# Two aggregating layers of a graph network: every second tile's hi and lo rows transposed by a DMA instead of TensorE

## What is computed

```python
h = layernorm(x)
for l in range(3):
    h_neigh = segment_sum(h[src], dst, n) / deg
    rst = relu(h @ W_self[l] + h_neigh @ W_neigh[l] + b[l])
    h = rst / max(sqrt(sum(rst * rst)), 1e-12)
x = x + h
x = x + ffn(layernorm(x))     # 8 experts, the best 2 of them by a gate
```

## Time and profile before

| what | value |
|---|---|
| time, median of 3 runs | 2151.08 us (2150.09 to 2151.2) |
| profiled execution, first to last instruction | 2150.1 us |
| PE busy | 2019.1 us (94%) |
| DVE busy | 1710.3 us (80%) |
| POOL busy | 1278.2 us (59%) |
| ACT busy | 1022.8 us (48%) |
| TensorE clock granted, mean | 0.985 of full speed |
| chain that ended last | PE 63%, POOL 11%, DVE 10%, issue 8%, ACT 4%, DMA 3% |

### The profile page before, as it was taken

The page is one execution under the profiler, slowest core; times in us unless marked ns, Lnnn a source line. Parts: engine busy times, 40 slices in busy tenths (PEclk is TensorE's granted clock), DMA queues, the critical chain, the costliest instruction groups (busy, mean ns, idle before and its releaser), DMA issues.

```text
span 2150.1 us, 44050 instructions
## 1 busy us (share of the span) xinstructions
PE 2019.1 (94%) x15237; PEld 1133.0 (53%) x15237; DVE 1710.3 (80%) x4183; ACT 1022.8 (48%) x1794; POOL 1278.2 (59%) x1396
## 2 busy tenths in 40 slices
PE   6999899997999999998999999987699989999996
PEld 3444444443444444443444444443477767777674
DVE  7678986655888888875888888875699989999985
ACT  4444333333334343443343343444677667766651
POOL 2884117664566666553444444444588888888865
PEclk9999999998999999999999999999999999999999
DMA  6664348964555555554666766665788997999874
GB/s 208 167 168 130 123 138 139 139 123 123 174 176 174 172 174 174 173 168 140 217 218 215 220 220 215 213 212 161 195 168 169 172 168 175 171 174 173 173 108 53
DMA packets 246210, 364.12 MB, mean 169 GB/s; under 512 B 115577, under 2 KB 115751, under 8 KB 245991
## 3 DMA queue, kind: packets, MB, share of 16 engines
q1 hardware_dynamic: 185175, 195.88, 35.9%
q0 software_dynamic: 60816, 165.43, 29.8%
HBM read 175.81 MB, written 165.31 MB: 159 GB/s over the span
## 4 chain that ended last, share of the span: by engine, by line
PE 63%; POOL 11%; DVE 10%; issue 8%; ACT 4%; DMA 3%; another core or an unknown queue 0%; SPq 0%; DVEq 0%; POOLq 0%; ACTq 0%
PE psS L523 26%; PE psY L523 25%; PE psT L1726 4%; POOL out_dram L861 2%; PE psY L1822 2%; POOL node_info L696 2%; PE psA L1781 2%; PE psA L1780 1%; POOL X L789 1%; DVE R L1429 1%; DMA w_n<-HH 1%; DMA w_s<-HH 1%; POOL G L773 1%; POOL zr L852 1%; POOL area L773 1%
## 5 line engine op out<-in xcount | busy, mean ns | idle before, releaser
L523 PE MATMUL psY<-w_n,HT 128*128 128x512 f16 x2664 | 616.6, 381 | 11.9 <-ACT HT L926 9.8
L523 PE MATMUL psS<-w_s,HT 128*128 128x512 f16 x2664 | 611.2, 379 | 1.0 <-DVE SB L1320 1.0
L523 PEld LDWEIGHTS psY<-w_n,HT 128*128 128x128 f16 x2664 | 260.7, 98 | 332.1 <-ACT HT L926 14.0
L523 PEld LDWEIGHTS psS<-w_s,HT 128*128 128x128 f16 x2664 | 251.5, 98 | 263.8 <-DVE SB L1320 1.2
L953 ACT ACTIVATE RR<-R 128x512 f32<-128x512 f32 x237 | 149.5, 631 | 303.4 <-DVE R L1429 299.4
L805 POOL DMA_INDIRECT y_rows<-YB,poutT x158 | 161.5, 1022 | 189.9 <-DVE YB L1308 157.9
L1320 DVE SCALAR_TENSOR_TENSOR SB<-psS,downs,bias 128x512 f32<-128x512 f32 x237 | 177.7, 750 | 76.8 <-PE psS L523 65.9
L798 POOL TENSOR_TENSOR scl<-ssm,halfpow 128x1 f32<-128x1 f32 x158 | 88.6, 561 | 239.3 <-DVE ssm L1447 239.2
L523 PE MATMUL psS<-w_w,raw 128*128 128x512 f16 x948 | 219.8, 382 | 0.8 <-ACT raw L1043 0.8
L1308 DVE SCALAR_TENSOR_TENSOR YB<-psY,YB 128x512 f16<-128x512 f32 x237 | 162.5, 686 | 55.6 <-ACT YB L919 46.8
L961 ACT ACTIVATE HH<-RR,scl 128x512 f16<-128x512 f32 x158 | 114.0, 722 | 150.1 <-POOL scl L798 150.1
(11 more groups left out here) (311 smaller groups left out, 3802.4 us busy)
## 6 DMA issues: line engine op xcount, KB each, us to landing
self_rows<-SB SPq DMA_DIRECT2D x236, 256.0 KB
Sl<-self_rows SPq DMA_DIRECT2D x158, 256.0 KB
area<-in_x_dram SPq DMA_DIRECT2D x78, 256.0 KB
y_rows<-YB SPq DMA_DIRECT2D x78, 256.0 KB
out_dram<-obb SPq DMA_DIRECT2D x78, 256.0 KB
raw<-in_L_gnn_W_neigh_dram SPq DMA_DIRECT2D x12, 256.0 KB
raw<-in_L_gnn_W_self_dram SPq DMA_DIRECT2D x12, 256.0 KB
y_rows<-YB,poutT POOLq DMA_INDIRECT x158
```

What stands on the lines that cost most here:

```text
L523: mm = eng.matmul(acc, lhs[:, a, c, :], w[:, bpart, c, :], start=(c == 0 and n == 0), stop=(stop and c == KC - 1 and n == 2))
```

## The change

For l = 1 and 2, an odd tile that is not late is turned by a transposing DMA that SP issues (`turn_rows`), straight from `HH` into one of four SBUF tiles `HTD` (the first four of `HTR`). PE's eight transposes and DVE's copy of that tile fall away. `turn_rows` stands in SP's steps with offset 1, ahead of `store_early`. `neigh` of such a tile waits for the DMA's landing (semaphores `hd`), and so does ACT's `hhi` of two tiles later, which writes the same `HH` buffer. The counts in the other waits are adapted, since PE turns fewer tiles. There are 37 such tiles in l = 1 (1 to 73) and 34 in l = 2 (1 to 67). The core of the diff:

```diff
+HD_RING = 4
+def by_dma(t, l):
+    return l in (1, 2) and t.t % 2 == 1 and late_place(t, l) is None
+def turned_by_dma(t):
+    before = t.run * len([k for k in range(T) if by_dma(Tile(k), 1)])
+    return before + len([k for k in range(t.t + 1) if by_dma(Tile(k), t.run + 1)])
+def turned_by_pe(t, l):
+    return t.n + 1 - (turned_by_dma(t) if l else 0)
...
+        HTD = HTR[0:HD_RING]
+        def dma_slot(t):
+            return (turned_by_dma(t) - 1) % HD_RING
+        def dma_landed(t):
+            return 16 * ((turned_by_dma(t) - 1) // HD_RING + 1)
...
             k = late_place(t, l)
+            if by_dma(t, l):
+                return HTD[dma_slot(t)]
...
+                def turn_rows(t, s=s, l=l):
+                    if not by_dma(t, l):
+                        return
+                    i = t.slot(2)
+                    sp.wait_ge(s.hhi, (t + 1).n)
+                    sp.wait_ge(s.hlo, (t + 1).n)
+                    if turned_by_dma(t) > HD_RING:
+                        sp.wait_ge(s.sp, (t + (1 - 2 * HD_RING)).n if t.t >= 2 * HD_RING else t.run * T)
+                    sp.dma_start_transpose(turned_rows(t, l).rearrange("p a c n -> p (a c) n"),
+                                           HH[i].rearrange("p a n -> p (a n)")).then_inc(s.hd[dma_slot(t)], 16)
-                    run_tiles(T, [(0, store_early)])
+                    run_tiles(T, [(1, turn_rows), (0, store_early)])
...
-                    run_plan(T, [(0, store_early), (5, load_self), (2, out_bias)],
+                    run_plan(T, [(1, turn_rows), (0, store_early), (5, load_self), (2, out_bias)],
...
-                after(act, s.tr, (t + -1).n)
+                if t.t >= 2 and by_dma(t + -2, l):
+                    act.wait_ge(s.hd[dma_slot(t + -2)], dma_landed(t + -2))
+                elif t.n >= 2:
+                    act.wait_ge(s.tr, turned_by_pe(t + -2 if t.t >= 2 else Tile(T - 2 + t.t, t.run - 1), l))
...
-                if late_place(t, l) is not None:
+                if late_place(t, l) is not None or by_dma(t, l):
                     return
...
-                after(pe, s.ht, (t + -1).n)
+                after(pe, s.ht, turned_by_pe(t, l) - (2 if l == 0 or late_place(t, l) else 1))
...
-                pe.wait_ge(s.ht, (t + 1).n)
+                if by_dma(t, l):
+                    pe.wait_ge(s.hd[dma_slot(t)], dma_landed(t))
+                else:
+                    pe.wait_ge(s.ht, turned_by_pe(t, l))
...
-                    if late_place(t, l) is None:
+                    if late_place(t, l) is None and not by_dma(t, l):
                         turn(t, l)
```

More of the change, by code:

```diff
@@ L194, in __init__ @@
         self.ht = sem("ht")
+        self.hd = [sem(f"hd{i}") for i in range(HD_RING)]
         self.y = sem("y")
@@ L971, in turn_late @@
                 s = ph[l]
-                act.wait_ge(s.tr, (t + 1).n)
+                act.wait_ge(s.tr, turned_by_pe(t, l))
                 act.activation(turned_rows(t, l), psT[t.slot(2)][:, :, :, :], ACT.Copy).then_inc(s.ht, 1)
@@ L1298, in turn @@
                 i = t.slot(2)
-                dve.wait_ge(s.tr, (t + 1).n)
+                dve.wait_ge(s.tr, turned_by_pe(t, l))
                 after(dve, s.sp, (t + -1).n)
```

## The result

The changed kernel takes 2498.44 us (median) against 2150.85 us of the kernel before in the same comparison: a ratio of 1.1616, 95% interval 1.1603 to 1.1629. It is 348 us slower. The forecast was 2427 us, slower, with 2275 to 2540 as the range. One of its six executions took 6316.16 us, why is not known, and stands outside the ratio. The profiled execution spans 2496.3 us.

A forecast was written before the change was run, and what follows sets the result against it. PE was taken to bound l = 1 and l = 2. Longer periods (63 + 140 us) and lower clock (26 + 47 us) add 276 us to 2150.1; with the median 1.0 us above the profiled span, 2427 us, range 2275 to 2540.

The forecast's parts named there:

- The ceiling of 31 us: On PE in l = 1 and l = 2: 71 odd tiles each lose 0.44 us of transposes, 31 us at most.
- SP's order: In SP's list the transposing DMA goes out behind a store, 10.27 us (l = 1) or 11.25 us (l = 2) after `neigh`.
- The landing: L, from transposing issue to waiting `neigh`: 3.6 us in l = 1, 5.1 in l = 2; longer periods add 63 and 140 us.
- The clock: PE's lower clock after idling costs 1.43 us: half of l = 1's pairs, 26 us; all of l = 2's, 47 us.
- the 51 us: Clock cost in l = 1 if, by the skill's rule, PE started slowly after every DMA wait; 25 us above the sum.
- The sum: Whole kernel: 63 + 140 + 26 + 47 = 276 us added to the profiled 2150.1 us.
- Costed at nothing: ACT's `hhi` wait, the ring of four, SP's 1.23 us issue and the even tiles' turning: no cost booked.
- The hidden landing (2120 us): Rival in l = 1 and l = 2: DMA lands in time, kernel 31 us faster, 2120 us; chance 0.05.
- The collision with gathers: Rival: DMA collides with POOL's gathers and scatters; 6.1 us landing in l = 1, 7.6 in l = 2; 2625 us, chance 0.08.
- The estimate of 10.5 us for eight blocks one after the other: Transposing DMA of one tile at the skill's 1309 ns per 128x128 block; the prediction noted the trace disagrees for most tiles.

The follow-up runs named there:

- early issues and the gather moved: Changed kernel with SP's transposing issue ahead of the store and, in l = 1, GpSimd's own-products gather ahead of its power of -0.5: 2130.41 us, ratio 0.9909.
- the early issue: Changed kernel with SP's transposing issue for tile u+2 moved ahead of the store of tile u, in both layers: 2146.71 us, ratio 0.9962.
- the kernel with all these tiles turned by DMA: Kernel with transposing issue ahead of the store and l = 1 gather moved, now turning all 143 tiles that are not late by DMA: 2118.6 us, ratio 0.9851.
- the gathers held apart: Changed kernel with GpSimd holding its next gathers until the tile's transposing DMA has landed: 2370.58 us; with l = 2's issue also ahead of load and bias: 2251.52 us.

## Why the prediction was right

**The ceiling of 31 us.** Right as a ceiling: with early issues and the gather moved, the pair takes 11.67 us in the median, 0.44 less than 12.11, and 22 us of the 31 are gained.

**SP's order.** Right, and the early issue shows that it decides: the same DMAs, 6 us earlier, and the kernel is faster than before. The issue came 613.86 - 601.88 = 11.98 us after `neigh`, the forecast's 10.27 and the 1.70 us of the slow matmuls. In l = 2 it came 1250.39 - 1237.43 = 12.96 us after it, the forecast's 11.25, 1.44 us of slow matmuls and 0.27 more.

**The landing.** The term mis-sized. L = 3.6 "near the short end" for l = 1 was 4.68 us on average: 36 x 1.08 = 39 us. I had looked at DMA shares and at SP's queue, and not at what GpSimd issues in the same instant: the gather at 613.55 stands in the old timeline at the same place in the step, just behind the store of 615.12:

```profile
615.24 1.07 POOL L789 DMA_INDIRECT Sl<-self_rows,pinT  x1 [0.19 <-issue]
```

Nor did most tiles of l = 3 land within 3.16 us, as the prediction has it. By the recorded updates of their semaphores, the 79 transposing DMAs of l = 3 in the kernel before took 2.9 to 9.0 us from issue to landing, 4.4 in the median; the choice of 3.6 lay below that. For l = 2, L = 5.1 was 4.83, 9 us less, and by the right cause, the transfers ahead on the queue, if not by it alone.

**The clock.** Right in kind and low in size: 26 us for l = 1 were 44 (27 of 37 `neigh` slow, not half), 47 us for l = 2 were 63 (34 of 34), each the sum of what the odd `neigh` took over 2.75 us. A slow `neigh` cost more than the 1.43 us booked, 1.6 us in l = 1 and 1.9 in l = 2. Part of it follows from the landing: PE stood idle for 3.1 us in l = 1 instead of the 2.2 forecast, and of the waits of some 2.06 us before the change 2 in 5 were followed by the lower clock, of those of 3.1 us 27 in 37. The section "HAM oscillation — how this bites in real kernels" of the Trainium skill's page "TensorE: Matmul & The Clock Gate" tells of the slow start after every wait for a DMA in a kernel whose waits are longer than the 2.2 us forecast here, so the 51 us that the prediction works out "by that rule" for l = 1 ask more of the page than it says. The trace has the slow start in l = 2 in every tile, after 3.9 to 4.9 us, in l = 1 in 27, and after waits of 1.58 us in 3 of 71.

**The sum.** 276 + 39 - 9 + 18 + 16 = 340 us, against 344 in the pairs. The two errors had one sign, and the range held them.

**Costed at nothing.** The traffic: right, PE was full beside it. ACT's `hhi` did wait for the landing, where I had it later: the instructions that waited for the transposing line, in the changed kernel, are (us in total, times)

```profile
  PE psY L551: 258.1, 71
  ACT HH L1003: 60.1, 37
```

34 of the 37 waits lie in l = 2. Nothing that shows followed from it, as DVE's lo half comes only after the copy of the even tile (there 1242.71 after 1242.10, with the hi half at 1237.49).

**The rivals.** The hidden landing (2120 us) was no outcome of this change, but the early issue with the gather moved comes near it, 2130 us: its condition, SP's order, was not met, and once it is met some 9 us are still lost. The collision with gathers came in part, at 4.7 us and not at 6.1. The estimate of 10.5 us for eight blocks one after the other, from the Trainium skill's page "VectorE: DVE Perf Modes", section "The three transpose paths", no run bears out: with the issue behind the store the landing took 3.2 to 5.2 us on average, and 6.3 us in l = 1 with the early issue. The advice of TensorE that the prediction cites with it stands in that page's section "Rules for kernel authors"; once the issue was early, the kernel with all these tiles turned by DMA was the fastest here, 2118.6 us.

## What to carry to other kernels

When a transfer is put into a queue that an engine works through in order, find what stands ahead of it there and what that waits for: data that had been ready for 6 us went out behind a store that waited for the end of the step, and the wait closed a loop through the whole step. Then list what every other queue issues within a microsecond or two of it: in l = 1 the same 256 KB took 3.3 us on average with the gathers held apart, 4.7 with one issued 0.3 us before, and 6.3 in the early issue, with two issued in the 1.4 us before. And count a wait on TensorE together with the clock that it costs.

## What had not been expected of the hardware

A transposing DMA of 256 KB took the same 4.7 to 4.8 us in two layers for different reasons, in l = 1 a gather started 0.3 us earlier, in l = 2 two transfers ahead on its queue and a gather, and 3.2 to 3.3 us once all were out of the way. In the early issue beside two gathers it took up to 8.0 us. And the clock followed the wait closely: with some 1.6 us of idle time in each pair nearly every `neigh` ran at full clock, with 3.1 us 27 of 37 were slow, with 3.5 us (l = 2 with the gathers apart) 33 of 34, with 3.9 to 4.9 us all 34.
